# Router logits in four column tiles whose halves the turning product adds, and the w2 and bias loads moved to SyncE's queue

## What is computed

```python
x = x + tanh(g_xattn[0]) * attention(layernorm(x), ctx, ctx)      # 16 heads of 16, causal, inside a tile
x = x + tanh(g_ffn[0]) * ffn(layernorm(x))

def ffn(x):                                   # xf: 8192 tokens x 256
    prob = softmax(xf @ w_router + b_router)  # 16 blocks of hidden units
    _, idx = top_k(prob, 4)
    mask = (idx[:, :, None] == arange(16)[None, None, :]).any(axis=1)
    h = relu(einsum('nd,ebd->neb', xf, w1b) + b1b)     # 16 blocks x 64 units
    return einsum('neb,ebd,ne->nd', h, w2b, mask) + b2
```

## Time and profile before

| | |
|---|---|
| median of 3 runs | 777.77 us (777.46 to 778.1) |
| the profiled execution | 777.98 us, of which the span of its instructions is 776.0 us |
| PE busy, PEld busy | 741.9 us (96%), 683.4 us (88%) |
| DVE, ACT, POOL busy | 556.8, 442.0, 487.4 us |

### The profile page before, as it was taken

The page is one execution under the profiler, slowest core; times in us unless marked ns, Lnnn a source line. Parts: engine busy times, 40 slices in busy tenths (PEclk is TensorE's granted clock), DMA queues, the critical chain, the costliest instruction groups (busy, mean ns, idle before and its releaser), DMA issues.

```text
span 776.0 us, 26862 instructions
## 1 busy us (share of the span) xinstructions
PE 741.9 (96%) x11496; PEld 683.4 (88%) x11496; DVE 556.8 (72%) x1363; ACT 442.0 (57%) x812; POOL 487.4 (63%) x663
## 2 busy tenths in 40 slices
PE   4579999999999999999999999999999999999888
PEld 3468999999999999999999999999999999999788
DVE  5388777877777777777777778778777777766552
ACT  1556566566556556556655655655665665565542
POOL 4686775576576566667657657656666765664542
PEclk9799999999999999999999999999999999999999
DMA  5111101111101111110111111011011011000001
GB/s 172 56 34 54 30 17 43 43 43 31 44 26 34 44 45 29 44 44 16 44 44 43 30 44 33 27 44 44 30 43 44 17 43 44 16 3 16 16 15 41
DMA packets 30116, 29.65 MB, mean 38 GB/s; under 512 B 3760, under 2 KB 29488, under 8 KB 30000
## 3 DMA queue, kind: packets, MB, share of 16 engines
q1 hardware_dynamic: 28576, 25.85, 10.6%
q10 hardware_dynamic: 1424, 2.10, 0.9%
HBM read 19.03 MB, written 8.39 MB: 35 GB/s over the span
## 4 chain that ended last, share of the span: by engine, by line
PE 92%; ACT 2%; DVE 2%; DMA 2%; issue 1%; ACTq 1%; POOL 0%; POOLq 0%; SPq 0%; DVEq 0%
PE score_banks L285 9%; PE score_banks L263 9%; PE bank L375 8%; PE bank L396 8%; PE bank L398 7%; PE bank L397 7%; PE bank L376 7%; PE bank L298 7%; PE bank L377 7%; PE bank L236 5%; PE bank L247 3%; PE bank L315 3%; PE bank L326 3%; PE bank L339 2%; PE score_banks L269 2%; ACT weights L451 1%
## 5 line engine op out<-in xcount | busy, mean ns | idle before, releaser
L694 POOL TENSOR_SCALAR_AFFINE_SELECT weights<-weights 128x1024 f32<-128x1024 f32 x128 | 137.7, 1100 | 120.4 <-ACT weights L451 120.4
L701 POOL TENSOR_TENSOR h_low<-hid,h_high 128x512 fp32r<-128x512 f32 x128 | 165.5, 1293 | 28.8 <-ACT hid L473 28.6
L549 DVE TENSOR_REDUCE q_pad<-score_banks 128x16 f32<-128x2048 f32 x64 | 146.0, 2282 | 14.6 <-PE score_banks L269 14.6
L602 DVE SCALAR_TENSOR_TENSOR hid<-bank,b_cols,used_all 128x256 f32<-128x256 f32 x248 | 108.1, 478 | 65.5 <-PE bank L377 60.5
L375 PE MATMUL bank<-xT_high,w_high 128*128 128x256 f32 x496 | 149.9, 302 | 0.0
L451 ACT ACTIVATE weights<-score_banks 128x1024 f32<-128x1024 f32 x128 | 124.3, 1024 | 37.1 <-PE score_banks L285 37.1
L396 PE MATMUL bank<-w_high,h_high 128*128 128x256 f32 x488 | 137.7, 282 | 3.6 <-DVE y_out L587 3.0
L376 PE MATMUL bank<-xT_low,w_high 128*128 128x256 f32 x496 | 139.4, 281 | 0.0
L377 PE MATMUL bank<-xT_high,w_low 128*128 128x256 f32 x496 | 139.3, 281 | 0.0
L398 PE MATMUL bank<-w_high,h_low 128*128 128x256 f32 x488 | 137.8, 282 | 0.0
L397 PE MATMUL bank<-w_low,h_high 128*128 128x256 f32 x488 | 137.6, 282 | 0.0
(11 more groups left out here) (90 smaller groups left out, 1400.5 us busy)
## 6 DMA issues: line engine op xcount, KB each, us to landing
c_in<-in_ctx SPq DMA_DIRECT2D x32, 256.0 KB, 2.8
x_in<-in_x SPq DMA_DIRECT2D x32, 256.0 KB, 3.1
out_y<-y_out SPq DMA_DIRECT2D x31, 256.0 KB, 2.1
w_stage<-in_w1T ACTq DMA_DIRECT2D x1, 1024.0 KB, 5.7
hid<-in_w2T ACTq DMA_DIRECT2D x8, 128.0 KB, 2.8
qT<-qT SPq DMA_DIRECT2D x64, 8.0 KB
out_y<-y_out SPq DMA_DIRECT2D x2, 128.0 KB, 1.7
b_all<-in_b SPq DMA_DIRECT2D x1, 128.0 KB, 4.8
```

What stands on the lines that cost most here:

```text
L549: dve.tensor_reduce(out=ride, in_=score_banks[:].rearrange("p u (r k) -> p u r k", k=S), axis=AX_X, op=ALU.max, negate=True).then_inc(max_ ...
L694: pool.affine_select(out=w, in_=w, compare_op=ALU.is_ge, fill=0.0, base=0, pattern=[[0, 2 * HB], [1, S]], channel_multiplier=-1).then_inc( ...
L701: pool.tensor_tensor(h_low[:, p % 2, chunks], hid[:, n % 4], h_high[:, p % 2, chunks].bitcast(F32), ALU.subtract).then_inc(h_low_made, 1)
```

## The change

The two chunks of the router's product no longer meet in PSUM. Each of the four products has its own column tile (0, 32, 64, 96) and its own rows, and ACT copies 128 rows. The transpose with the identity becomes a plain fp32 product with the matrix `adding` (128 x 64), which has ones where a row's chunk and block meet the tile and block of a column, so that it turns and adds the two halves at once. DVE makes `adding` once at i = 1. The bias is loaded to the rows of chunk 0 alone. The eight w2 loads leave ACT's queue and are issued by SP, four behind `max_row(0)` and four behind `max_row(1)`; the eight bias loads, two in each of iterations 0 to 3 before, go four behind `max_row(2)` and four behind `max_row(3)`. The pieces of w2 are split in iterations 2 and 3 and no longer in 1 and 2.

```diff
-        br_rows = sb("br_rows", [PAIR * PAD, 1], F32)
+        br_rows = sb("br_rows", [P, 1], F32)
+        adding = sb("adding", [P, PAIR, PAD], F32)
...
-        logitT = sb("logitT", [PAIR * PAD, S], F32)
+        logitT = sb("logitT", [P, S], F32)
...
         def pieces_of(i):
-            n = 2 * (i + 1)
-            return range(n, n + 2) if 0 <= n < 8 else ()
+            n = {-1: 0, 0: 2, 2: 4, 3: 6}.get(i, 8)
+            return range(n, n + 2) if n < 8 else ()
...
-                for c in range(KC):
-                    for t in range(PAIR):
-                        rows = slice(t * PAD, (t + 1) * PAD)
+                for t in range(PAIR):
+                    for c in range(KC):
+                        rows = slice((t * KC + c) * PAD, (t * KC + c + 1) * PAD)
                         made = pe.matmul(out=banks[M1][rows, 0:S], lhsT=w_router[:, c, :], rhs=xT[:, c, t, :],
-                                         start=c == 0, stop=c == KC - 1, tile_position=(0, rows.start))
+                                         start=True, stop=True, tile_position=(0, rows.start))
...
             def logits_transposed(p):
+                if p == 0:
+                    pe.wait_ge(adding_made, 1)
                 pe.wait_ge(route_copied, p + 1)
-                pe.transpose(banks[M1][:, 0:PAIR * PAD], logitT[:], ident[0:PAIR * PAD, 0:PAIR * PAD]).then_inc(route_turned, 1)
+                pe.matmul(out=banks[M1][:, 0:PAIR * PAD], lhsT=logitT[:], rhs=adding[:].rearrange("p t e -> p (t e)"),
+                          start=True, stop=True).then_inc(route_turned, 1)
...
-                if i == -1:
-                    for c in range(HC):
-                        act.dma_start(w2_stage[:, c], A_w2T.rearrange("(e c r) n -> e c r n", c=HC, r=UNITS)[:, c]
-                                      ).then_inc(w_landed[1], 16)
...
-                    act.activation(logitT[:], banks[M1][0:PAIR * PAD, 0:S], ACT.Identity, bias=br_rows[:]).then_inc(route_copied, 1)
+                    act.activation(logitT[:], banks[M1][:, 0:S], ACT.Identity, bias=br_rows[:]).then_inc(route_copied, 1)
...
+                    dve.wait_ge(ident_made, 1)
+                    halves = ident[:].rearrange("p (t c e) -> p t c e", c=KC, e=PAD)
+                    dve.tensor_tensor(adding[:], halves[:, :, 0], halves[:, :, 1], ALU.add).then_inc(adding_made, 1)
...
-                if 0 <= i < HC // 2:
-                    for c in range(2 * i, 2 * i + 2):
+                if 0 <= i < HC // 4:
+                    for c in range(4 * i, 4 * i + 4):
+                        sync.dma_start(w2_stage[:, c], A_w2T.rearrange("(e c r) n -> e c r n", c=HC, r=UNITS)[:, c]
+                                       ).then_inc(w_landed[1], 16)
+                if HC // 4 <= i < HC // 2:
+                    for c in range(4 * i - HC, 4 * i - HC + 4):
                         sync.dma_start(b1_cols[:, c:c + 1], A_b1.rearrange("(e c r) -> e c r", c=HC, r=UNITS)[:, c].unsqueeze(2),
                                        allow_slow_non_contiguous=True).then_inc(b1_landed, 16)
```

More of the change, by code:

```diff
@@ L162, in build @@
             "top_found", "clipped_made", "clipped_found", "marked_made"))
-        gated_b2_made = sem("gated_b2_made")
+        gated_b2_made, adding_made = sem("gated_b2_made"), sem("adding_made")
         ident16_zeroed, ident16_made, ident_zeroed, ident_made = (sem(n) for n in (
@@ L777, in _ @@
             for t in range(PAIR):
-                rows = slice(t * PAD, t * PAD + BLOCKS)
+                rows = slice(t * KC * PAD, t * KC * PAD + BLOCKS)
                 sync.dma_start(br_rows[rows], A_b_router.rearrange("(e o) -> e o", o=1)).then_inc(br_landed, 16)
```

## The result

The changed kernel takes 765.17 us (median of 4 runs, 764.32 to 766.09) against 777.62 us. The ratio is 0.9839, 95% interval 0.9822 to 0.9856: 12.5 us, or 1.6%, faster. The forecast was 760.6 us with a range of 757 to 768. The time lies in that range, but not in the 758 to 763 us that the forecast as summed had for itself, and the gain is about three quarters of the one forecast (12.5 of 17.0 us). The profiled execution took 764.39 us, its span 762.6 us, 13.4 us less than before.

The account below looks back on a forecast made before the run. PE was taken as the bound, holding 92% of the chain. 777.98 - 4.4 - 2.5 + 0.2 - 6.4 - 4.1 = 760.8 us profiled, so 760.6 us median; range 757 to 768, own range 758 to 763.

Parts of the forecast that it names:

- The bound: PE holds 92% of the chain; in the steady part only time off PE's own order counts, the start has waits.
- term 1: Start, ACT's queue: without the eight w2 issues ACT copies q earlier, first shifted scores at 19.35 not 23.79; -4.4 us.
- Term 2: Start, PE's clock: with a shorter pause the clock keeps its level through the serial chain; -2.5 us, other end 0.
- The first rival: Start: PE's clock falls all the same, the router's and turning gains stay; 763.1 us, chance 0.17.
- Term 3: Loads on SP cost nothing; the later split of w2 pieces delays POOL in iteration 3; +0.2 us, bounds 0 and 1.6.
- Terms 4 and 5: Router iterations: four column tiles for the router's products, -0.22 us a pair; turning product with 128 rows, -0.14 us a pair.
- The product as dear as four passes: Turning product takes four passes, 0.67 us instead of 0.57, losing 2.9 us; 767.6 us, chance 0.10.
- four tiles that bring nothing: Router: L298's first passes already fill the two idle tiles beside L339; 767.0 us, chance 0.05.
- a drained PE: Turning product drains PE before, between and after its passes, 1.35 us instead of 0.57; 787.5 us, chance 0.03.
- The start's gain was taken back: Late splits of pieces 6 and 7 or SP's w2 issues hold up later steps; about 765 to 768 us, chance 0.05.
- the slower rival: Slower than before, because the turning product drains PE around its passes, 0.78 us a pair; 787.5 us, chance 0.03.
- Those for the router and the period: Eight records after L339 in about 0.4 us, four starting at once; 1.22 us to L285; two-iteration period down 0.36 us.

Follow-up runs that it names:

- awake: Changed kernel plus 14 identity transposes to an unused bank in each of PE's two long pauses at the start; 760.93 us.
- before_awake: Kernel before plus identity transposes on PE, 52 ahead of the first shifted scores and 14 ahead of the scores of iteration 1; 776.15 us.
- early_split: Changed kernel with all eight w2 loads behind the first row of maxima and the pieces split in iterations 1 and 2 as before; 763.02 us.
- rows128: Kernel before with logitT at 128 rows, upper 64 zeros, turned by one fp32 transpose; the router keeps two column tiles; 768.94 us.
- plain64: Kernel before with the turning made by a plain fp32 product with the 64 x 64 identity, still 64 rows; 782.80 us.
- sum_in_psum: Changed kernel with the fillers of `awake`, one 128-row transpose in place of the product with `adding`, and DVE adding the halves into PSUM; 757.37 us.
- busy_longer: `sum_in_psum` with 8 more filler transposes ahead of the scores of each of iterations 2, 3 and 4; 757.16 us.
- router_only: Changed kernel with the old places of w2 and bias loads and splits, so only the router's part is changed; 767.64 us.
- dve_adds: Changed kernel with the fillers of `awake`, loads and splits of `early_split`, one 128-row transpose, and DVE adding the halves into SBUF; 758.15 us.

## Why the prediction was right, and where it was off

- **The bound and term 1 were right.** The first shifted scores start at 19.25 us, forecast 19.35; 4.5 us and not 4.4. No other wait showed up there.
- **Term 2 failed**, at the words "I take 2.5". The clock fell again, to 0.50 up to 31.4 us, and instead of 2.5 us gained, 1.0 was lost: from the first to the third row of shifted scores it took 18.87 us (17.89 before). The low stretch of 10.24 us had covered PE's pause and the first shifted scores; now it began after these were done and reached the attention output (1.93 us, 1.08 before) and the second shifted scores (2.04 us, 1.17 before). The first rival had the mechanism (its 763.1 supposed that nothing more is lost). `awake` shows it: with the clock kept, the kernel has 760.93 us, and the forecast was 760.6; `before_awake` shows the same 2.5 us in the kernel before. The error was to weigh two ends by how near the busy share was to a stretch that had kept its clock, when no row lay between.
- **Term 3 was right in kind and too small.** The w2 issues on SP held up nothing (2.57 us for four). The late split cost 0.5 us and not 0.2, within its bounds; `early_split` takes it back in the trace.
- **Terms 4 and 5 were right.** Forecast 0.22 + 0.14 = 0.36 us a pair; the period is 0.360 us shorter, 0.21 from the router's products and 0.15 from the turning. From the 6th row of shifted scores to the end it is 10.4 us less than before, forecast 10.5. `rows128` and `plain64` show that the pauses came with the 64 rows, as argued from the earlier trace rows, and `rows128` against `sum_in_psum` gives 0.206 us for the four tiles. Whether a part of this comes from no longer adding the chunks in PSUM was not varied.
- **The sum.** -4.5 + 1.0 + 0.5 - 10.4 = -13.4 us, which is the whole difference of the spans. Of the 3.8 us that are missing from the -17.2 forecast, 3.5 are term 2. No other error made up for it; the time is in the wide range because that was drawn to take in the rivals. The median is 0.8 us above the profiled execution, because two of the four runs took 766.0 us.
- **Rivals.** The product as dear as four passes, four tiles that bring nothing, a drained PE: none appeared. The start's gain was taken back in part, by the clock and the late split. (The 787.5 us of the slower rival is counted from the profiled execution, the other rivals from the median, 0.2 us less.)
- **Signs.** Those for the router and the period came. A stretch at 0.50 behind L285's start was not to be there, and was. And one sign of being wrong did appear: the first 60 us end 3.0 us earlier (the 6th row of shifted scores at 62.30 and not 65.32), under the 4 us named.

## What to carry to other kernels

Where one engine holds the chain for hundreds of us, count starts from one group to the next, not busy time: 0.36 us a pair came out to the hundredth, 0.21 of it from two column tiles that had stood empty and 0.15 from a group that used half of the rows and had pauses around it. Giving an odd small product the full 128 rows can be worth more than giving it fewer passes (0.30 us of the period in `rows128`, 0.15 for one record instead of two). And when a change shortens a pause of PE, what the clock does afterwards is a term of its own, larger here than all others that were off; put work in the pause and measure it.

## What was not expected of the hardware

- PE's clock fell at 21.15 us though PE had been busy for 2.40 of the 6.50 us around it, and in `sum_in_psum` after 2.69 busy of 4.60 us, while `awake` kept it after 3.01 of 4.60, and so did `busy_longer` after only 2.61 of the same 4.60. So the busy share of such a stretch does not tell here whether the clock falls. In the changed kernel it then stayed at 0.50 for 10.2 us with PE busy 8.14 of them, and in `router_only` for 13.6.
- Executions of one program differ by the same cause in part: the kernel before took 777.2 to 777.8 us where the granted clock was 0.993, and 779.1 to 779.7 where it was 0.991 or 0.989 (11 runs). It is not all: one run of `awake` took 762.61 us at 1.000, four took 760.7 to 760.9. The rest is open.
- Two small DVE instructions took 1.98 us and not 0.38 while POOL worked and their operands lay in SBUF alone. Of the 64 clippings of `dve_adds` three were slow (0.93 and 1.13 us at this place, 1.28 at 717.92), each begun while POOL was already at an instruction and ended within 0.03 us of the end of one; the others took 0.22 to 0.24. In `sum_in_psum`, where the source is in PSUM, five clippings began with at least 0.7 us of a POOL instruction to come and took 0.23 each. So it took both, POOL at work and all operands in SBUF; why is not shown.
